# After the last panel GpSimd makes half of the spread moves, two square roots stand ahead of copies on ScalarE, and the later terms are not cleared

## The reference, cut to what matters

```python
u = par_u[0] * par_u[1] * (diag_u[:, None] * ego_u @ W_u) + ego_u      # 2048 rows
i = par_i[0] * par_i[1] * (diag_i[:, None] * ego_i @ W_i) + ego_i      # 3072 rows
e = jnp.concatenate([u, i], axis=0)
h = adj @ (adj.T @ e)
out = (h - mu) * jax.lax.rsqrt(var + LN_EPS) * ln_gamma + ln_beta + res
x = _layernorm(x + out)
# second layer: four Chebyshev terms, K = 4
Tx_prev1 = L_scaled @ x                        # L_scaled is adj
for k in range(2, K):
    Tx_curr = 2.0 * (L_scaled @ Tx_prev1) - Tx_prev2
    out = out + Tx_curr @ weight[k]
x = _layernorm(x + out + bias)
```

## Time and profile before

| What | Value |
|---|---|
| Time, median of 3 runs | 1176.56 us (1174.76 to 1181.24) |
| Time of the profiled execution | 1176.35 us |
| Its span in the trace | 1174.5 us |
| TensorE, busy share of the span | 92% |
| VectorE | 77% |
| ScalarE | 29% |
| GpSimd | 23% |
| Transfers | 340.33 MB, 290 GB/s mean |

### The profile page before, as it was taken

How to read it: one execution, slowest core, us unless ns; L and a number is a source line. 1 busy time by engine, 2 the same in 40 slices (tenths; PEclk the granted TensorE clock), 3 DMA queues, 4 the chain that set the end, 5 groups by cost and what they waited for, 6 DMA issues and landing times.

```text
span 1174.5 us, 13988 instructions
## 1 busy us (share of the span) xinstructions
PE 1083.6 (92%) x5040; PEld 468.9 (40%) x5050; DVE 909.4 (77%) x942; ACT 335.8 (29%) x600; POOL 264.4 (23%) x421
## 2 busy tenths in 40 slices
PE   6899999999999999677889999999899999988897
PEld 5444444444444444322333333443344444423332
DVE  2798798999989989598777776665586777668885
ACT  1556546645645645500111110100110100011111
POOL 0476645545435434420000000000000000001110
PEclk9999999999999999899999999999999999989999
DMA  9999999999999995999999999999799999999991
GB/s 277 273 277 301 294 273 316 297 306 276 281 295 281 278 293 144 214 246 346 275 347 347 333 328 310 303 289 261 191 291 344 335 340 348 342 282 342 346 339 27
DMA packets 366970, 340.33 MB, mean 290 GB/s; under 512 B 17500, under 2 KB 365700, under 8 KB 366932
## 3 DMA queue, kind: packets, MB, share of 16 engines
q1 hardware_dynamic: 257972, 232.24, 70.6%
q10 hardware_dynamic: 106496, 105.00, 30.8%
q0 software_dynamic: 2464, 2.59, 0.9%
HBM read 338.48 MB, written 1.31 MB: 289 GB/s over the span
## 4 chain that ended last, share of the span: by engine, by line
PE 55%; DVE 13%; SPq 12%; ACT 10%; issue 5%; ACTq 2%; POOL 2%; DMA 1%; DVEq 0%; POOLq 0%
PE bank L1258 26%; ACT terms L834 9%; SPq L377 7%; DVE turned L549 6%; PE bank L1326 5%; SPq L366 5%; PE bank L1271 5%; PE bank L1128 2%; PE bank L1088 2%; PE bank L1116 2%; PE bank L1140 2%; PE bank L1100 2%; DVE shared L569 2%; ACTq L320 1%; PE bank L1304 1%
## 5 line engine op out<-in xcount | busy, mean ns | idle before, releaser
L432 POOL COPY raw<-raw 32x512 f32<-32x512 f32 x320 | 195.6, 611 | 241.6 <-DVE raw L586 200.5
L1258 PE MATMUL bank<-turned,terms 128*128 128x512 f32 x528 | 235.5, 597 | 3.2 <-DVE turned L549 2.7
L569 DVE STREAM_TRANSPOSE shared<-shared 32x512 f32<-32x512 f32 x320 | 224.0, 700 | 4.1
L1088 PE MATMUL bank<-shared 128*64 128x256 f32 x1600 | 206.8, 387 | 9.5 <-DMA shared<-in_adj 9.3
L549 DVE STREAM_TRANSPOSE turned<-shared 128x2048 f32<-128x2048 f32 x70 | 160.2, 2301 | 60.2 <-PE bank L1258 34.2
L549 DVE STREAM_TRANSPOSE turned<-raw 128x2048 f32<-128x2048 f32 x70 | 159.7, 2296 | 52.2 <-PE bank L1258 37.4
L834 ACT COPY terms<-terms 32x512 f32<-32x512 f32 x320 | 197.0, 616 | 5.1 <-DVE terms L579 0.9
L325 POOL DMA_DIRECT2D out<-scratch x32 | 17.4, 552 | 596.8 <-DVE scratch L781 596.6
L1258 PEld LDWEIGHTS bank<-turned,terms 128*128 128x128 f32 x528 | 97.9, 190 | 131.1 <-issue 129.1
L1088 PEld LDWEIGHTS bank<-shared 128*64 128x64 f32 x1600 | 112.0, 137 | 92.8 <-issue 33.7
L1326 PE MATMUL bank<-turned,terms 128*64 128x512 f32 x360 | 97.0, 603 | 23.7 <-DVE turned L549 22.7
(11 more groups left out here) (157 smaller groups left out, 1074.5 us busy)
## 6 DMA issues: line engine op xcount, KB each, us to landing
shared<-in_adj SPq DMA_DIRECT2D x100, 1024.0 KB, 10.7
raw<-in_adj SPq DMA_DIRECT2D x100, 512.0 KB, 10.9
raw<-in_adj ACTq DMA_DIRECT2D x100, 512.0 KB, 12.7
shared<-in_adj SPq DMA_DIRECT2D x100, 512.0 KB, 10.4
shared<-in_adj ACTq DMA_DIRECT2D x100, 512.0 KB, 12.3
raw<-in_adj SPq DMA_DIRECT2D x80, 256.0 KB, 7.6
shared<-in_x SPq DMA_DIRECT2D x5, 256.0 KB, 4.7
xq<-in_x POOLq DMA_DIRECT2D x40, 32.0 KB, 6.1
```

The lines of the kernel that those rows point to most:

```text
L432: last = nc.gpsimd.tensor_copy(moved[Q32 * c:Q32 * (c + 1), :, :, Q32 * q:Q32 * (q + 1)], beside[Q32 * q:Q32 * (q + 1), :, c, :, :])
L569: last = nc.vector.transpose(low_turned[Q32 * c:Q32 * (c + 1), :, :, Q32 * q:Q32 * (q + 1)], low[Q32 * q:Q32 * (q + 1), :, :, Q32 * c:Q32 ...
L1088: last = nc.tensor.matmul(t_bank[H * odd:H * (odd + 1), 0:PW], e[:, s * SB + b, :], panels[slot][:, s * SB + b, :], start=(k == 0 and b < ...
L1258: last = nc.tensor.matmul(sum_bank[parity][:, :], terms[:, c * GB + i, columns], turned[place][:, i * BANK:(i + 1) * BANK], start=(first a ...
```

## The change: what it does

```diff
@@ GpSimd, behind the last panel's moves @@
+            pool.wait_ge(across_made, NJ)
+            pool.wait_ge(spread_used, NJ)
+            for block in range(NQ * NQ // 2, NQ * NQ):
+                q, c = block // NQ, block % NQ
+                last = nc.gpsimd.tensor_copy(spread[Q32 * c:Q32 * (c + 1), :, :, Q32 * q:Q32 * (q + 1)],
+                                             across[Q32 * q:Q32 * (q + 1), :, c, :, :])
+            last.then_inc(spread_helped, 1)
+            pool.wait_ge(spread_helped, 1)
+
             pool.wait_ge(tile_used, TURNED + T1)
-            pool.wait_ge(spread_used, NJ + 1)
-            nc.gpsimd.memset(terms[:, :, H:3 * H], 0.0).then_inc(zeroed, 1)
             nc.gpsimd.memset(scratch[0:H, 2:4, :], 0.0).then_inc(zeroed, 1)
@@ ScalarE @@
-            def spread_across(j, first, end):
+            def spread_across(j, first, end, signal=NQ * NQ):
...
-                if end == NQ * NQ:
+                if end == signal:
                     last.then_inc(spread_made, 1)
...
             root(0, 2 * GB)
-            spread_across(NJ, 4, 8)
+            spread_across(NJ, 4, NQ * NQ // 2, NQ * NQ // 2)
+            root(1, 2 * GB)
             take_y(1, SEGS[1])
             load_next()
-            root(1, 2 * GB)
-            spread_across(NJ, 8, NQ * NQ)
             take_h(2, SEGS[2])
             load_next()
             take_y(2, SEGS[2])
             take_h(3, SEGS[3])
+            root(2, 2 * GB)
             take_y(3, SEGS[3])
-            root(2, 2 * GB)
             take_h(NS - 1, SEGS[-1])
             root(3, 2 * GB)
             take_y(NS - 1, SEGS[-1])
@@ TensorE @@
                 elif k == ACROSS:
+                    if cc == 0:
+                        pe.wait_ge(spread_helped, 1)
                     add_h_spread(1, cc, NJ, cc == PB - 1)
...
-                pe.wait_ge(zeroed, 3)
+                pe.wait_ge(zeroed, 2)
...
-            pe.wait_ge(zeroed, 2)
```

More of the change, by code:

```diff
@@ L182, in resnorm_chebyshev @@
         spread_used = sem("spread_used")
+        spread_helped = sem("spread_helped")
         t_summed = sem("t_summed")
```

## The result

The changed kernel takes 1171.03 us (median of 7 executions, 1168.52 to 1177.02), the kernel before 1180.57 us (7 executions, 1172.36 to 1182.84, measured with it). The ratio is 0.994, with a 95% interval of 0.9914 to 0.9966: about 7 us faster (the medians lie 9.5 us apart, the means 6.8). The forecast, 1166.4 us against 1176.35 for the profiled execution, was 10.0 us. The profiled execution after the change took 1168.52 us with a span of 1166.7, 7.8 us less; it is the fastest of the seven.

What follows compares the result with a forecast made beforehand. TensorE was taken to bound most of the kernel, VectorE the second layer's start; 4.9 + 1.7 + 3.3 + 0.1 = 10.0 us saved at tile 2 gave 1166.4 against 1176.35 us, range 1164.0 to 1171.5.

Steps and rivals of the forecast that it cites:

- Which arms: Between the layers: spread, root and clearing arms end together behind GpSimd's moves; none is worth its length by itself.
- When the spread is whole: GpSimd's eight new moves end at 483.1, so TensorE's spread product starts there instead of 488.03: 4.9 us saved.
- Collisions throughout: Rival, 0.13: all eight GpSimd moves take 1.16 us, the spread is whole at 486.5, time 1171.5 us.
- third four: ScalarE's moves from 475.42 to 477.92, said to complete its half of the spread and not to be late.
- Root(2) ahead of take_y(3): On ScalarE, root(2) follows take_h(3) directly and comes at 487.8: 3.3 us saved.
- The variance: VectorE's input for root(2), forecast ready at about 487.0, 0.8 us before ScalarE comes.
- The clearing: Without GpSimd's clearing of `terms`, the residual starts right behind VectorE's scaling: 0.1 us saved, bounds 0 and 0.23.
- the sum: All four savings reach VectorE's tile 2 and last to the end: 4.9 + 1.7 + 3.3 + 0.1 = 10.0 us.
- TensorE's clock: TensorE stands still only 0.6 us and keeps full clock between the spread's two halves: 1.7 us saved.
- the clock falls anyway: Rival, 0.14: TensorE's clock falls despite the short stop, the 1.7 us are lost again, time 1168.1 us.
- The transfers: Rival, 0.06: load transfers, not VectorE, set the pace in the second layer; with seven late loads, 1185 us.

Runs made afterwards that it cites:

- roots_back: The changed kernel with both roots back behind ScalarE's copies; VectorE's tile 2 came at +19.90 us of the stretch, against +18.71 after the change.
- the second: The changed kernel timed again (12 executions) against the kernel before (17): 1172.55 against 1177.77 us, ratio 0.9963.
- the better version: The changed kernel with turn_h(4) in tile 1, six moves on GpSimd and root(4) ahead of take_y(4): 1166.78 us, ratio to before 0.9906.
- the last one: The better version with root(7) ahead of ScalarE's part of load 8: 1167.15 us, ratio to before 0.9916.

## Why the prediction was right, and where it failed

**Which arms.** Right. The roots and the clearing give nothing alone, and taken out of the whole they cost 1.2 and 1.6 us. That is what arms of like length do. One part the prediction did not see: in the kernel with the moves alone the clearing worked on VectorE too (2.57 us for 0.17).

**When the spread is whole.** Right, and by its reason. The product was forecast 4.9 us earlier and came 11.14 - 6.34 = 4.8 earlier in the stretch. Three of the eight moves took 0.95, 0.97 and 1.01 us, the others about 0.61; TensorE waited 0.79, with 0.6 forecast. Collisions throughout, the rival, are excluded. (ScalarE's moves from 475.42 on, "third four" in the prediction, are its second four; the sum does not hang on it.) The Trainium skill's rule (page "SBUF — State Buffer", section "Who interferes with whom") names the right pair. Blocking for the whole instruction, which the page spells out for another kind of VectorE operation (its two-port modes) and the prediction took for this pair, would be 0.69 us; the trace has 0.34 to 0.55 on the move and 0.29 or nothing on the operation.

**Root(2) ahead of take_y(3).** Right: forecast at 487.8, it came at 487.49 on ScalarE and 487.79 on VectorE. The variance was forecast at 487.0; VectorE had it 1.38 us before it got the root, at 486.4. What root(1) is worth by itself was not measured: `roots_back` moves both roots, and there VectorE waited 1.29 us for root(2), so its own steps were not on the path.

**The clearing.** Right: nothing by itself, with 0.1 forecast, and its weight beside the others was 1.6 us.

**The step that failed** is the sum, which let the arms' gains arrive whole at tile 2: "4.9 + 1.7 + 3.3 + 0.1 = 10.0 us for VectorE's tile 2". The terms were each found in the first profile, and VectorE was ready at 493.41 where I said 493.6, but tile 2 needs the place that tile 0 leaves. The prediction followed ScalarE's and GpSimd's arms to VectorE and put TensorE's own work behind the spread at nothing, 12.3 us without a stop, with `turn_h(4)` in the middle of tile 0. That cost 1.84 us, and moving `turn_h(4)` away took the wait off. By the stretch 8.0 us came, and 8.38 by the starts of tile 2, which were 8.39 at tile 100; 7.8 us reached the end. The 0.6 between is in the last stretch (341.02 us from tile 100 to the end, before 340.46), which differs by more than that between executions of one kernel. This is the account of the fastest execution; over all of them about 7 us came in the first comparison and 4.4 in the second. Besides the 1.84 us the profiles show one more loss, the clock's, next.

**TensorE's clock.** The second term that did not hold. The 1.7 us came in one profile of the change and were lost in the other, of 1.5 us (tile 2 at +18.71 and +20.18). So the rival "the clock falls anyway", at 0.14, is what happens in some executions; in how many, two profiles do not tell. The prediction took the stop as 0.6 us because it let `turn_h(1)` run at half clock as before; that it did so in the first profile (2.63 us) was luck. Where it ran at full clock, TensorE was done sooner and stood 2.36 and 2.38 us; its clock fell in the one case and not in the other.

**The transfers.** VectorE never got slower than before for them. In the better version, 2.8 us ahead at tile 3, roots behind ScalarE's issues made VectorE wait, and 2.1 of the 2.8 us were gone at tile 20. That the transfers are the limit behind these issues fits the longer landings, but is not shown.

**What stays open.** The stretch gained 6.0 to 8.0 us between the two profiles of each kernel, 0.5 to 0.7%; the first comparison says 0.6%, the second 0.37% with an interval up to 0.56%. Whether the changed kernel loses its clock more often late in the second layer is not settled: from tile 100 to the end its profiles took 341.02 and 344.93 us, those of before 340.46 and 341.47, and before with one edit of its start 344.53 and 344.31.

## What to carry to other kernels

Where several arms end together, follow each to the buffer that the last step writes, and add the engine that is busiest anyway: the arm that never waits shows no wait in the trace of before and is the next bound. An edit that earns nothing alone can be worth something beside the others, so test it by taking it out of the whole. And where a kernel's time differs by more from one execution to the next than the change is worth, measure the stretch that is changed, not the whole, and in more than one profile: here one profile of the change was 1.5 us better than the next.

## What was unexpected on the chip

- One issue of a load's part took ScalarE 0.3 to 0.8 us between 500 and 535 us of before, up to 3.42 us there in the better version and 4.65 in the last one. It is nothing new in kind: every profile, that of before too, has issues of over 5 us later (5.31 us at 864 us, with 348 GB/s).
- The same program has its clock falls in other places from one execution to the next. Between 1060 and 1120 us the change's first profile was granted the full clock in each window, and its second 0.91 to 0.98 (the two fences, same columns as above); from 1020 to 1040 it is the other way about, 0.83 and 0.99:

```profile
1060.00:1080.00 20.00, 16.83 (x77) 5.77 (x78) 17.67 (x15) 1.57 (x4) 4.35 (x8) 1.00 1.10 348
1100.00:1120.00 20.00, 17.34 (x74) 5.55 (x72) 15.36 (x14) 3.89 (x8) 2.17 (x4) 1.00 1.10 341
```

```profile
1060.00:1080.00 20.00, 17.59 (x75) 6.45 (x76) 14.08 (x17) 1.95 (x5) 4.35 (x8) 0.93 1.10 337
1100.00:1120.00 20.00, 17.59 (x72) 5.96 (x72) 18.60 (x16) 2.65 (x5) 3.20 (x6) 0.91 1.10 349
```

- A GpSimd move of 0.61 us took 0.95 to 1.16 beside a VectorE operation with two inputs, and some of those operations 0.98 instead of 0.69 (L699, L700), others still 0.69 (L695, L711): a partial loss.
- A VectorE step of 0.17 us (TENSOR_SCALAR, 128x8) took 0.37 to 0.40 beside such moves, which lost nothing by it, and 2.57 beside GpSimd's clearing.
